# Relational passes of a graph network: eight one-hot marks of a pair made by two long VectorE instructions, and one more check in the preparation

## What is computed

```python
def _rgcn_layer(h, src, dst, et, W, root_w, b, N):
    xw = jnp.einsum('ni,rio->rno', h, W)                  # 8 relations
    cnt = jnp.zeros((W.shape[0], N), h.dtype).at[et, dst].add(1.0)
    msg = xw[et, src] / cnt[et, dst][:, None]
    agg = jax.ops.segment_sum(msg, dst, num_segments=N)
    return agg + h @ root_w + b
...
for l in range(hop):                                      # hop = 2
    h = _rgcn_layer(out, src, dst, et, W, root[l], bias[l], N)
    h = jnp.maximum(h, 0.0) if l < hop - 1 else h
    out = 0.5 * out + 0.5 * h
```

## Time and profile before

| what | us |
|---|---|
| median of 3 runs | 5106.49 |
| lowest and highest run | 5106.47, 5111.46 |
| span of the profiled execution, first to last instruction | 5889.7 |
| first relational pass in it, 1545 to 2800 | 1255 |
| second relational pass in it, 2800 to 4014 | 1214 |
| attention loop and end in it, 4500 to 5889 | 1389 |

### The profile page before, as it was taken

The page is one execution under the profiler, slowest core; times in us unless marked ns, Lnnn a source line. Parts: engine busy times, 40 slices in busy tenths (PEclk is TensorE's granted clock), DMA queues, the critical chain, the costliest instruction groups (busy, mean ns, idle before and its releaser), DMA issues.

```text
span 5889.7 us, 68338 instructions
## 1 busy us (share of the span) xinstructions
PE 3488.8 (59%) x18857; PEld 2347.3 (40%) x18858; DVE 2346.7 (40%) x6053; ACT 1356.1 (23%) x2994; POOL 2262.0 (38%) x2340
## 2 busy tenths in 40 slices
PE   5599996998633334333333333337995566566566
PEld 3255553444422223222232332333444455445445
DVE  7756566114322222222122222223116555555556
ACT  2555451001200000000000000001003555555555
POOL 3000001000366666665666666661002444444442
PEclk8699998999756665666555555557996677777767
DMA  2111113222522222222111111113220222122112
GB/s 70 52 68 46 67 45 130 92 87 91 156 56 69 66 68 65 65 69 66 45 46 45 45 45 46 46 43 121 87 109 16 43 45 44 41 43 45 45 41 57
DMA packets 264711, 371.66 MB, mean 63 GB/s; under 512 B 63251, under 2 KB 200250, under 8 KB 256298
## 3 DMA queue, kind: packets, MB, share of 16 engines
q1 hardware_dynamic: 186790, 251.51, 12.8%
q0 software_dynamic: 74464, 114.31, 8.5%
q10 hardware_dynamic: 3364, 4.69, 0.3%
HBM read 261.10 MB, written 109.21 MB: 63 GB/s over the span
## 4 chain that ended last, share of the span: by engine, by line
PE 21%; issue 17%; another core or an unknown queue 13%; DVE 8%; POOL 8%; DVEq 6%; DMA 1%; ACT 1%; ACTq 0%; POOLq 0%; SPq 0%
POOL GS L719 8%; PE psum L1375 7%; PE psum L1535 5%; DVEq L1877 3%; DVE GS L1877 3%; PE psum L1321 3%; PE psum L1562 2%; DMA GS<-xw_table,stage 1%; DVEq L1884 1%; PE psum L1468 1%; PE psum L1469 1%; PE psum L1529 1%; PE psum L1300 1%; DVE O L2514 0%
## 5 line engine op out<-in xcount | busy, mean ns | idle before, releaser
L719 POOL DMA_INDIRECT GS<-xw_table,stage x1664 | 1574.4, 946 | 1444.9 <-issue 1075.0
L1375 PE MATMUL psum<-HA,HT 128*128 128x512 fp8e4 (+1 forms) x5733 | 1251.5, 369 | 54.2 <-DVE HT L2060 54.2
L1321 PE MATMUL psum<-GS 128*128 128x96 f32 x3328 | 688.6, 383 | 652.7 <-DMA GS<-xw_table,stage 576.6
L1321 PEld LDWEIGHTS psum<-GS 128*128 128x128 f32 x3328 | 635.2, 289 | 701.6 <-issue 698.2
L719 POOL DMA_INDIRECT HA<-p_table,stage x624 | 602.1, 965 | 734.4 <-ACT stage L1085 509.2
L1375 PEld LDWEIGHTS psum<-HA,HT 128*128 128x128 bf16 x5733 | 554.0, 100 | 632.5 <-DVE HT L2060 55.2
L1877 DVE TENSOR_SCALAR GS<-iota,HT,wt 128x96 f32<-128x96 f32 x1680 | 473.4, 348 | 454.9 <-issue 453.3
L1891 DVE TENSOR_TENSOR HA<-HA,psum 128x96 f32 x208 | 52.8, 254 | 1388.2 <-remote 964.7
L1300 PE MATMUL psum<-Wcat,HT 128*128 128x512 f32 x196 | 177.1, 1057 | 459.9 <-DVE HT L2349 410.7
L1039 ACT ACTIVATE HA<-psum 128x392 fp8e4<-128x392 f32 x784 | 349.4, 494 | 344.0 <-PE psum L1280 331.2
L815 ACT ACTIVATE stage<-edge_cols 128x16 int32 (+1 forms) x104 | 22.2, 216 | 1551.1 <-PE psum L1321 693.6
(11 more groups left out here) (383 smaller groups left out, 4221.3 us busy)
## 6 DMA issues: line engine op xcount, KB each, us to landing
HT<-dst_rows SPq DMA_DIRECT2D x212, 256.0 KB
xw_table<-HT SPq DMA_DIRECT2D x100, 512.0 KB, 3.2
HA<-adj SPq DMA_DIRECT2D x26, 1600.0 KB, 6.4
adj<-HA SPq DMA_DIRECT2D x13, 3136.0 KB, 9.5
HA<-adj SPq DMA_DIRECT2D x26, 1536.0 KB, 9.7
GS<-xw_table,stage POOLq DMA_INDIRECT x1664
HA<-p_table,stage POOLq DMA_INDIRECT x624
h_table<-HA SPq DMA_DIRECT2D x4, 960.0 KB, 5.6
```

The source lines that it names most:

```text
L719: nc.gpsimd.indirect_dma_start(out=to, out_offset=None, in_=table, in_offset=bass.IndirectOffsetOnAxis(ap=idx, axis=0)).then_inc(done, 16)
L1321: last = nc.tensor.matmul(bank[h][:, 0:WINDOW], G3[g][:, j, :], S_pair[h][:, t, :], start=(t == 0), stop=(t == 2 * GT - 1))
L1375: last = nc.tensor.matmul(bank[s][:, 0:w], Hs4[:, b, t, :], adj_tile[s][:, b * GW:b * GW + w], start=(b == 0 and t == 0), stop=(b == SRCS ...
```

## The change

`windows` makes the marks of a pair by two instructions over all 8 tiles (768 elements of each partition): the first compares the column numbers, broadcast over the tiles, with the destinations, broadcast over the columns; the second multiplies the result in place by the weights, broadcast over the columns. Between the two stands a wait for the first. Both count up `windows_ready`, so TensorE's threshold for a pair is twice what it was. In the preparation, `flags` gets a sixth check (three short instructions over 208 groups) and the maximum is taken over six columns.

```diff
@@ TensorE, sum_pass
-                        pe.wait_ge(windows_ready, (PAIRS + 1) * l + k + 1)
+                        pe.wait_ge(windows_ready, ((PAIRS + 1) * l + k + 1) * 2)
@@ VectorE, sum_pass
                 def windows(k, s):
-                    for j in range(2 * GT):
-                        last = V.tensor_scalar(S_pair[s][:, j, :], iota[:, 0:WINDOW], dl_pair[:, bass.ds(k * 2 * GT + j, 1)],
-                                               wt[:, bass.ds(k * 2 * GT + j, 1)], ALU.is_equal, ALU.mult)
-                    last.then_inc(windows_ready, 1)
+                    at = k * (2 * GT) if isinstance(k, int) else dve.snap(k * (2 * GT), min_val=0, max_val=COLS - 2 * GT)
+                    spread = lambda t: t[:, bass.ds(at, 2 * GT)].unsqueeze(2).broadcast_to([P, 2 * GT, WINDOW])
+                    V.tensor_tensor(S_pair[s], iota[:, 0:WINDOW].unsqueeze(1).broadcast_to([P, 2 * GT, WINDOW]), spread(dl_pair),
+                                    ALU.is_equal).then_inc(windows_ready, 1)
+                    dve.wait_ge(windows_ready, ((PAIRS + 1) * l + k) * 2 + 1)
+                    V.tensor_tensor(S_pair[s], S_pair[s], spread(wt), ALU.mult).then_inc(windows_ready, 1)
@@ VectorE, flags
                 top(4, hi_pair[:, 0:PAIRS])
-                ch(V.reduce_max(two_flags[:, 0:1], flag1[:, 0:5], AX.X))
+                ch(V.scalar_tensor_tensor(of_group, lo, -4.0, iota[:, 0:GROUPS], ALU.mult, ALU.add))
+                ch(V.tensor_scalar(of_group, of_group, 4.0 * LAG, None, ALU.is_ge))
+                top(5, of_group)
+                ch(V.reduce_max(two_flags[:, 0:1], flag1[:, 0:6], AX.X))
```

## The result

| | us |
|---|---|
| before, median of 4 runs (lowest, highest) | 5107.84 (5106.47, 5111.46) |
| changed, median of 4 runs (lowest, highest) | 5148.85 (5147.05, 5152.82) |
| ratio, 95% interval | 1.0081 (1.0068 to 1.0093) |
| forecast, range | 5217, 5095 to 5300 |

The account below looks back on a forecast made before the run. The prediction took POOL's gathers to bound the timed passes. Held gathers 112 us, old marks' effect minus 2 and sixth check plus 1 gave +111 on 5106.5: 5217 us, range 5095 to 5300, chance of slower 0.66.

Parts of the forecast that it names:

- The bound: Timed relational passes are bound by POOL's gathers: 1.25 us a step, 20.0 us an iteration; VectorE has slack.
- The lengths: Each new VectorE marks instruction of 768 elements takes 0.96 us; two and a step make 1.95 us, hidden under slack.
- The hold: In the passes, a running VectorE instruction with two SBUF inputs holds POOL's gather until it ends: 0.54 us a pair.
- the term of 112 us: Cost of held gathers on POOL in the passes: 0.54 us a pair for 208 pairs, averaged over all phases.
- The surplus of the first profile: The profiled execution's 783 us (15%) over the timed runs was read as delays from recording each instruction.
- the gathers' floor: Least time of the two relational passes at POOL's gather pace: 104 iterations of 20.0 us, 2084 us.
- The rival of slow register operations: Slow register operations of VectorE's marks also pace timed passes, so fewer of them give 4835 us, faster; chance 0.17.
- the no-change rival: Gathers in the passes are not held, or POOL's waits for buffers absorb it: 5106 us; chance 0.17.
- The sixth check: Three short instructions added to VectorE's chain in the preparation: 1.1 us more, all counted.
- The old marks' 2 us: Old marks slowed gathers of the passes by 1 ns each over 1664; the change removes this, minus 2 us.

Follow-up runs that it names:

- the kernel cut in two: The changed kernel with each long instruction of the marks cut into two of four tiles (384 elements each): 5135.3 us, ratio 1.0051 against the kernel before.

## Why the prediction was right, and where it was wrong

**The bound: right.** The timed passes are POOL's gathers, 1.25 us each. With the sixth check alone they take 2102.4 us from the first start to the last, where 1663 steps of 1.25 are 2079 and the 22.0 us in which POOL stands idle between the passes are nearly all. Five more marks a pair cost nothing.

**The lengths: right.** 0.96 us forecast, 956 and 962 ns measured (957 the median of both).

**The hold: the mechanism right, the size wrong.** A gather that meets a running instruction of two SBUF inputs is held, as forecast. The steps that failed are the two from which the term of 112 us was made: "So a gather has one moment, 0.13 us after its start (0.945 less 0.82), at which a running instruction of this kind holds it until that instruction ends", and "all u from 0 to 1.25 are alike". Together they gave 0.54 us a pair. The trace has 0.20 us a pair, 42 us over 208 pairs. The end of a hold was as forecast; the beginning of the window, the gap and the phase (how long after VectorE's instruction a gather starts) were not, as the timeline of the changed kernel shows.

```profile
1644.34 1.03 DVE L1881 TENSOR_TENSOR GS<-GS,wt 128x768 f32<-128x768 f32 x1
1644.38 0.94 POOL L719 DMA_INDIRECT GS<-xw_table,stage  x1 [0.30 <-issue]
...
2004.46 0.96 DVE L1878 TENSOR_TENSOR GS<-iota,HT 128x768 f32<-128x768 f32 x1 [1.14 <-issue]
2004.56 1.68 POOL L719 DMA_INDIRECT GS<-xw_table,stage  x1 [0.30 <-issue]
2005.56 0.96 DVE L1881 TENSOR_TENSOR GS<-GS,wt 128x768 f32<-128x768 f32 x1
2006.54 0.94 POOL L719 DMA_INDIRECT GS<-xw_table,stage  x1 [0.30 <-issue]
...
2107.25 0.95 POOL L719 DMA_INDIRECT GS<-xw_table,stage  x1 [0.30 <-issue]
2107.42 0.96 DVE L1878 TENSOR_TENSOR GS<-iota,HT 128x768 f32<-128x768 f32 x1 [1.13 <-issue]
2108.50 0.94 POOL L719 DMA_INDIRECT GS<-xw_table,stage  x1 [0.30 <-issue]
2108.52 0.97 DVE L1881 TENSOR_TENSOR GS<-GS,wt 128x768 f32<-128x768 f32 x1
...
2116.53 0.95 DVE L1878 TENSOR_TENSOR GS<-iota,HT 128x768 f32<-128x768 f32 x1
2117.24 1.05 POOL L719 DMA_INDIRECT GS<-xw_table,stage  x1 [0.30 <-issue]
...
2250.10 0.96 DVE L1878 TENSOR_TENSOR GS<-iota,HT 128x768 f32<-128x768 f32 x1 [1.14 <-issue]
2250.20 1.67 POOL L719 DMA_INDIRECT GS<-xw_table,stage  x1 [0.30 <-issue]
```

*The end of a hold.* The gather at 2004.56 ends at 2006.24, and the one at 2117.24 at 2118.29: each 0.81 to 0.82 us after the end of the instruction that it met (2005.42, 2117.48), as in the earlier trace rows. In terms of starts, a gather that begins v after a long instruction is held for 0.83 - v: 0.73 us at v = 0.10, 0.11 us at v = 0.71. All 108 gathers that start with v between 0.04 and 0.83 us are held, and by that length to 0.02 us.

*The beginning of the window.* The prediction held a gather that starts up to 0.13 us ahead of the instruction, at the highest price of all. The trace doesn't: of the 135 gathers that begin in the 0.2 us ahead of either instruction (as at 2108.50 above, 0.02 us ahead) the longest took 36 ns more. The last start that is not held comes at v = 0.037 us (1644.38 above), the first that is held at 0.045. So the window is v from about 0.04 to 0.83 us (the expectations have it as 0.03 to 0.82): 0.79 us wide, the hold 0.79 us at most. Whether a gather is held is thus settled at its own start, not 0.13 us later, and what the prediction read as a moment 0.13 us inside the gather fits as well with a hold that ends 0.13 us ahead of the instruction's end; which of the two it is at that end, no row tells. The row of before that was used, a start 0.15 us ahead that was not held, fitted either reading, and the prediction had no row closer to the start.

*The gap between the two instructions* is 0.14 us (2005.42 to 2005.56), not 0.03. This matters little to VectorE. But a gather that the first instruction held starts its successor 0.83 + 1.25 = 2.08 us after the pair's beginning, past the second one's window, so mostly only one of the two can hit.

With the window and the gap as measured, and still all phases alike, the first instruction costs 0.79² / 2 = 0.31 us and the second 0.15 x 0.72 = 0.11 us (only the starts 1.14 to 1.29 us after the first one's beginning reach its window without having been held), both over 1.25: 0.34 us a pair, 70 us. So 42 of the missing 70 us are the window and the gap.

*The phase* is the rest, 70 to 42 us. Summed by place, a pair is held for 0.37 us in the first half of an iteration and 0.18 in the second half in the first pass, 0.18 and 0.07 us in the second pass, where an even spread gives 0.34. Only the first of these places is spread out: its next gather starts anywhere from 0.02 to 1.24 us after the first long instruction (the pairs at 2004.46 and 2250.10 are two of this place). In the other three the distance hardly moves: 0.57 to 0.75 us in 46 of 53 pairs (second half, first pass), 1.00 to 1.18 us in 45 of 52 (first half, second pass), and 0.85 to 1.01 us in 47 of 53 (second half, second pass). VectorE's marks are started by matmuls, which are started by gathers; and these three distances happen to be cheap, near the window's end or behind it, which is luck and no property of the change. The prediction had said that the phase is not really free, and averaged all the same, over four places. The experiments show what the phase is worth: 41, 72 and 110 us for the same two instructions with nothing, one memset and two memsets ahead. The first long instruction starts 0.40 us after the first memset with one (2262.22 to 2262.62 in a row below), 0.68 us with two, not the 0.48 and 0.7 us that the expectations moved it by, as it begins before the memset has ended.

(A slip of the prediction without effect: 0.96 of 1.25 is 0.768, not 0.765.)

**The surplus of the first profile: a right use with a wrong cause.** The step was: "I read these as delays of the profiled execution, which writes a record for each instruction". Seven profiled executions with spans of 5104 to 5214 us, as long as their timed runs, were recorded in the same way; and timed runs of the kernel before took 5852, 5855 and 5860 us in three series. So the surplus is no cost of being profiled but a condition in which a kernel's runs, timed or profiled, take 15% more. One and the same chip had it in one series and not in a later one: 5852 and 5112 us for the kernel before. The timed runs to be predicted were not in it, so taking their passes at the gathers' floor was right.

**The rival of slow register operations** (4835 us) falls twice. In the profiled executions that are as long as the timed runs there are none (118 ns at most with the old marks). And in the condition in which there are, two thirds fewer sequencer instructions give next to nothing. Three kernels of one such series show it: the kernel before, the one with both memsets and both operands in PSUM, and the one with one memset (gathers' row, then POOL's idle time before them: us, times):

```profile
L719 POOL DMA_INDIRECT GS<-xw_table,stage x1664: 938/944/1027, 1550.4 to 3975.7; - x185
...
  remote: 251.5, 75
  PE psum L1321: 103.3, 65
```

```profile
L720 POOL DMA_INDIRECT GS<-xw_table,stage x1664: 938/944/1047, 1550.7 to 3971.9; - x185
...
  remote: 250.7, 74
  PE psum L1322: 98.4, 61
```

```profile
L719 POOL DMA_INDIRECT GS<-xw_table,stage x1664: 938/944/2157, 1552.9 to 3970.7; - x185
...
  PE psum L1321: 157.5, 79
  remote: 100.3, 40
```

The second holds no gather (1571.7 us busy against 1573.2) and has few register operations, so it shows what these are worth: from the first gather to the last 2421.2 us against 2425.3, 4 us and not 273. In the third, gathers are held for longer, 1658.9 against 1573.2 us busy, 86 us; its waits for buffers and "remote" are shorter by 97 us, and its passes take 2417.8 us. Where POOL waits anyway, a held gather costs nothing: the mechanism of the no-change rival is real, only the timed runs to be predicted were not in that condition.

**The small terms.** The sixth check was forecast at 1.1 us and measured 0.7, inside its interval of some 5 us. The old marks' 2 us: with an operand in PSUM, 1.9 us less than before, likewise too small to tell (the gathers' busy time is 4.8 us less than with the old marks).

## What to carry to other kernels

Where POOL sets the pace with indirect gathers, a VectorE instruction with two SBUF inputs beside them is not free even on an idle VectorE: here each gather that began 0.04 to 0.83 us after the start of a 0.96 us instruction was held by it. Put one operand in PSUM, use the form with one tensor and per-partition scalars, or cut the instruction shorter. And when a cost depends on how two periodic engines meet, an even average is only a guess: look up, in each place of the loop, what starts the one and how long after the other, since a delay of 0.4 us on an engine with slack here cost 31 us. Last, before a profiled execution that is much longer than the timed runs is explained, take a second profile.

## What the runs showed of the hardware that was not expected

*The hold begins sharply, after the instruction's start, and it goes both ways.* A gather that starts ahead of a `tensor_tensor` of two SBUF inputs, or less than some 0.04 us after its start, is not held; one that starts just after that loses 0.79 us. In the first case it is VectorE's instruction that becomes longer: 0.97 us with the gather 0.02 us ahead, 1.00 at v = 0.006, 1.03 at v = 0.037 (the row at 1644.34), where 0.957 is the median. There were 37 such, 1.3 us in all, on an engine with slack. The Trainium skill (SBUF — State Buffer, section Who interferes with whom) says that a second SBUF input goes through the shared read interface, and, of VectorE's two-port modes, that the one that issues first has the ports for its whole instruction. The experiment with operands in PSUM agrees on the inputs, and the lengths above agree that the first one goes ahead and the other waits. The whole length is not what a gather can lose, though: it is 0.79 of 0.96 us, and 0.39 of 0.55 us in the kernel cut in two. The section's inference that `tensor_tensor` leaves descriptor generation alone is not what these gathers show.

*A one-input instruction directly ahead of such an instruction widens the window.* With one memset ahead, all 12 gathers that began up to 0.34 us ahead of the `tensor_tensor`, so during the memset, were held through both (the kernel with one memset, timeline):

```profile
2262.22 0.48 DVE L1878 MEMSET rows<- 128x512 f32 x1 [1.16 <-issue]
2262.29 2.04 POOL L719 DMA_INDIRECT GS<-xw_table,stage  x1 [0.31 <-issue]
2262.62 0.89 DVE L1879 TENSOR_TENSOR GS<-iota,HT 128x768 f32<-128x768 f32 x1
2263.66 0.96 DVE L1882 TENSOR_TENSOR GS<-GS,wt 128x768 f32<-128x768 f32 x1
```

The gather ends at 2264.33, 0.82 us after the first long instruction's end. Of 16 that began 0.35 to 0.42 us ahead, about when the memset did, one was held. The memset does nothing of the kind alone: ahead of marks with operands in PSUM, 77 and 23 gathers started during the first and the second memset, and the longest took 956 ns. Why the window is wider then stays open. It accounts for what the count had missed: with the window of the change and the true delays of 0.40 and 0.68 us the same reckoning gives about 60 and 100 us, and the traces have 73 and 109 us of held time (each gather over 945 ns, summed); in the first of them the 13 gathers held from ahead of the instruction make up 13 us. The expectation of 72 us for one memset had a delay that was too long and a window that was too narrow, and the two errors cancelled.

*A condition of 15% more time.* Split by the stages, with the kernel that has the sixth check alone first and the kernel before in the long condition second:

```profile
core 0: us, PE busy (x) PEld busy (x) DVE busy (x) ACT busy (x) POOL busy (x), PEclk, DMA share, GB/s
0.00:1545.00 1545.00, 1320.88 (x6868) 720.01 (x6869) 813.44 (x1845) 501.29 (x1143) 71.12 (x50) 0.93 0.24 84
1545.00:3651.00 2106.00, 984.04 (x3661) 787.49 (x3661) 572.42 (x2165) 63.75 (x200) 1574.79 (x1664) 0.54 0.24 64
3651.00:5110.00 1459.00, 1176.72 (x8328) 841.06 (x8328) 928.31 (x2046) 788.58 (x1651) 619.80 (x626) 0.83 0.28 73
```

```profile
0.00:1549.00 1549.00, 1322.06 (x6868) 721.86 (x6869) 812.88 (x1842) 502.34 (x1143) 72.14 (x50) 0.93 0.24 84
1549.00:3978.00 2429.00, 892.49 (x3661) 722.28 (x3661) 609.53 (x2164) 63.43 (x200) 1573.16 (x1664) 0.56 0.21 56
3978.00:5841.00 1863.00, 1282.74 (x8328) 903.44 (x8328) 934.70 (x2047) 791.13 (x1651) 620.45 (x626) 0.78 0.21 57
```

The preparation takes 1545 and 1549 us; the passes 323 us more, the attention loop 404 us more, at a granted clock that is no lower in the passes (0.56 against 0.54) and a little lower in the loop (0.78 against 0.83). Both of these stretches are loops, and in the first of them single register operations of line 1877 take up to 1397 ns where 118 was the longest. What brings the condition on was not found: it held for all kernels of a series, in three series on three chips, and was absent in three others, one of them on a chip that had had it.
